# A two-layer decoder: scattering additions by tile, expert stores on another queue, a context term made once an entry

## What is computed

```python
# layer 0, routed experts: 8 experts, each takes up to 640 tokens (top 2 of the router)
hmid = relu(einsum('ceh,ehi->cei', inputs_tokens, experts_inter))
out = einsum('cei,eih->ceh', hmid, experts_out)
combined = zeros((T, h)).at[used_tokens].add((out * weights).reshape(-1, h))

# layer 1, coattention: c is x, q is the context, 77 rows
cq = einsum('bcd,bqd,d->bcq', c, q, w_cq) + b_cq
s = (c @ w_c + b_c)[:, :, None] + (q @ w_q + b_q)[:, None, :] + cq
a = softmax(s, axis=2)
b_att = softmax(max(s, axis=2), axis=1)

# layer 1, gated experts: 16 experts, each takes 32 tokens of every entry
h = gelu(einsum('becd,edf->becf', expert_in, w1) + b1)
expert_out = einsum('becf,efd->becd', h, w2) + b2
out = out.at[arange(b)[:, None, None], idx].add(gates[..., None] * expert_out)
```

## Time and profile before

| what | value |
|---|---|
| median of 3 runs | 2429.12 us (2428.93 to 2432.93) |
| the profiled execution, its own time | 2436.9 us |
| its span, first to last instruction | 2435.0 us |
| TensorE busy, of the span | 2087.2 us, 86% |
| VectorE, ScalarE, GpSimd busy | 64%, 52%, 46% |
| mean granted TensorE clock | 0.933 of full speed |
| routed experts | about 820 to 1059 us of the span |
| coattention | about 1416 to 1597 us |
| gated experts | about 1687 us to the end |

### The profile page before, as it was taken

How to read it: one execution, slowest core, us unless ns; L and a number is a source line. 1 busy time by engine, 2 the same in 40 slices (tenths; PEclk the granted TensorE clock), 3 DMA queues, 4 the chain that set the end, 5 groups by cost and what they waited for, 6 DMA issues and landing times. The chain is left out here.

```text
span 2435.0 us, 47109 instructions
## 1 busy us (share of the span) xinstructions
PE 2087.2 (86%) x17414; PEld 1478.5 (61%) x17446; DVE 1565.7 (64%) x3061; ACT 1267.3 (52%) x2042; POOL 1126.5 (46%) x1292
## 2 busy tenths in 40 slices
PE   7599999995995499948999979951999999999995
PEld 5466666663663388735666668841667676676664
DVE  5488888875896655537888746666554554555542
ACT  2366666663443355626666634432664655646642
POOL 2988888841220243236665213301454554545533
PEclk9799999997998699979999969975999999999998
DMA  5000000000002233211111000041343444444422
GB/s 223 1 2 1 0 0 0 0 1 6 10 6 70 93 127 144 76 37 36 27 26 26 1 14 16 13 138 72 104 95 100 95 106 97 84 103 104 102 47 33
DMA packets 63078, 135.99 MB, mean 56 GB/s; under 512 B 11201, under 2 KB 47249, under 8 KB 56081
## 3 DMA queue, kind: packets, MB, share of 16 engines
q0 software_dynamic: 31488, 52.45, 10.8%
q1 hardware_dynamic: 31504, 82.41, 9.7%
HBM read 100.22 MB, written 34.60 MB: 55 GB/s over the span
## 5 line engine op out<-in xcount | busy, mean ns | idle before, releaser
L3354 ACT ACTIVATE f_h<-bank,f_b 128x512 f32<-128x512 f32 x256 | 175.9, 687 | 276.3 <-PE bank L176 269.0
L3397 DVE TENSOR_TENSOR f_hidlo<-f_h,f_hidhi 128x512 f16<-128x512 f32 x256 | 177.2, 693 | 169.1 <-ACT f_hidhi L3355 169.1
L176 PE MATMUL ring<-f_w2hi,f_hidhi 128*128 128x256 f16 x1024 | 279.2, 273 | 6.3 <-DVE f_hidlo L3397 4.1
L176 PE MATMUL ring<-f_w2hi,f_hidlo 128*128 128x256 f16 x1024 | 279.1, 273 | 0.0
L176 PE MATMUL ring<-f_w2lo,f_hidhi 128*128 128x256 f16 x1024 | 279.1, 273 | 0.0
L3453 POOL DMA_INDIRECT out<-f_y,f_to_row x128 | 212.0, 1656 | 47.5 <-issue 34.1
L176 PE MATMUL bank<-f_xthi,f_w1hi 128*128 128x512 f16 x512 | 194.7, 380 | 0.0
L176 PE MATMUL bank<-f_xtlo,f_w1hi 128*128 128x512 f16 x512 | 194.6, 380 | 0.0
L176 PE MATMUL bank<-f_xthi,f_w1lo 128*128 128x512 f16 x512 | 194.6, 380 | 0.0
L3355 ACT ACTIVATE f_hidhi<-bank,f_b 128x512 f16<-128x512 f32 x256 | 173.9, 679 | 0.0
L3439 POOL DMA_INDIRECT f_xg<-tokens,f_from_row x128 | 149.6, 1169 | 47.9 <-issue 34.5
(11 more groups left out here) (620 smaller groups left out, 6047.9 us busy)
## 6 DMA issues: line engine op xcount, KB each, us to landing
f_raw<-in_e_w SPq DMA_DIRECT2D x32, 1024.0 KB, 4.9
c_raw<-in_e_w SPq DMA_DIRECT2D x16, 1024.0 KB, 4.9
slots_out<-c_y POOLq DMA_DIRECT2D x40, 128.0 KB, 3.5
x<-in_x SPq DMA_DIRECT2D x1, 4096.0 KB
tokens<-c_xn SPq DMA_DIRECT2D x16, 256.0 KB, 2.6
tokens<-f_xn SPq DMA_DIRECT2D x16, 256.0 KB, 2.4
out<-x SPq DMA_DIRECT2D x1, 4096.0 KB, 14.3
wb<-in_wb SPq DMA_DIRECT2D x1, 3096.0 KB, 33.0
```

The source lines that it names most:

```text
L176: mm = pe.matmul(out, left[a], right[b], start=first and n == 0, stop=last and n == 2)
L3354: act.activation(h32[n % 4][:, :], src, ACT.Gelu_apprx_tanh, bias=bias).then_inc(sig["h_full"], 1)
L3397: dve.tensor_tensor(hid_v[1][:, it, at], h32[n % 4][:, :], hid_v[0][:, it, at], ALU.subtract).then_inc(sig["h_lo"], 1)
```

## The change

It has three edits. In the gated experts GpSimd waits for the tile that it is about to add, not for all eight, and copies `to_row` ahead of that. In the routed experts the stores are issued by SyncE, woven between the loads of the expert after next; VectorE waits for `y_stored` itself, and `y_free` falls away. In coattention the context's term is made once per twin, by two matmuls at the head of the pair, into columns of their own in the same bank (`by_context`); ScalarE copies them to SBUF (`row`), and VectorE adds them with the biases while it takes `similar`. TensorE waits for `row_ready` ahead of `similar`.

```diff
--- before.py
+++ after.py
@@ -1946,13 +1946,32 @@
         with nc.Block() as block:
             @block.sync
             def _(sp):
-                def load(p, e, more):
+                def load_w1(e):
                     sp.wait_ge(sig["w1_split"], e.before)
                     sp.dma_start(raw1[:, :], dram["e0_w1"][bass.ds(e.before * P, P), :]).then_inc(sig["w1_loaded"], 16)
+                def load_w2(e):
                     sp.wait_ge(sig["w2_split"], e.before)
                     sp.dma_start(raw2[:, :], dram["e0_w2"][bass.ds(e.before * P, P), :]).then_inc(sig["w2_loaded"], 16)
 
-                each_expert(sp, E0, load)
+                def expert(p, e, more):
+                    after = Turn(value(sp, e.before + 2), value(sp, e.before + 3)) if more == 2 else None
+                    if after:
+                        load_w1(after)
+                    for ct in range(CT):
+                        sp.wait_ge(sig["y_read"], e.count(CT, ct + 1))
+                        sp.dma_start(dram["slots_out"][bass.ds(e.before * CAP0 + ct * P, P), :],
+                                     tiles(y[p][:, :], CT)[:, ct, :]).then_inc(sig["y_stored"], 16)
+                        if ct == 0 and after:
+                            load_w2(after)
+                for e in (Turn(0, 1), Turn(1, 2)):
+                    load_w1(e)
+                    load_w2(e)
+                each_expert(sp, E0, expert)
+                sp.wait_ge(sig["y_stored"], 16 * E0 * CT)
 
             @block.tensor
             def _(pe):
@@ -2067,7 +2086,7 @@
                         after = Turn(e.now, e.now + 1)
                         low_slots(after)
                         low_w1(after)
-                    dve.wait_ge(sig["y_free"], e.before)
+                    dve.wait_ge(sig["y_stored"], e.count(16 * CT, 0))
                     for ct in range(CT):
                         dve.wait_ge(sig["y_made"], e.count(CT, ct + 1))
                         dve.tensor_copy(y[p][:, ct * D:(ct + 1) * D], bank[4 + ct % 4][:, 0:D]
@@ -2099,18 +2118,10 @@
                 def expert(p, e, more):
                     if more == 2:
                         gather(Turn(e.after, e.after + 1))
-                    pool.wait_ge(sig["y_stored"], e.count(16 * CT, 0))
-                    pool.sem_inc(sig["y_free"], 1)
-                    for ct in range(CT):
-                        pool.wait_ge(sig["y_read"], e.count(CT, ct + 1))
-                        settle(pool, sig)
-                        pool.dma_start(dram["slots_out"][bass.ds(e.before * CAP0 + ct * P, P), :],
-                                       tiles(y[p][:, :], CT)[:, ct, :]).then_inc(sig["y_stored"], 16)
 
                 gather(Turn(0, 1), first=True)
                 gather(Turn(1, 2))
                 each_expert(pool, E0, expert)
-                pool.wait_ge(sig["y_stored"], 16 * E0 * CT)
 def linear_attention(nc, mem, dram):
 
 
@@ -2738,7 +2749,7 @@
             u = Twin(sig, p)
             u.bank = mem.banks[4 * p:4 * p + 4]
             u.c_t, u.c_n, u.sim_w = sb("c_t", KT * CTX), sb("c_n", D), sb("sim_w", KT * CTX)
-            u.a, u.a_t = sb("a", NT * CTX), sb("a_t", S)
+            u.a, u.a_t, u.row = sb("a", NT * CTX), sb("a_t", S), sb("row", CTX)
             u.neg_peak, u.total = sb("neg_peak", NT), sb("total", NT)
             u.top, u.e_row, u.e_sum = sb("top", 1), sb("e_row", S), sb("e_sum", 1)
             u.b_col, u.q2c, u.tmp = sb("b_col", NT), sb("q2c", KT), sb("tmp", W2)
@@ -2754,6 +2765,7 @@
             u.turned, u.peak_row = u.bank[0], u.bank[0][0:1, 0:S]
             u.b_out, u.q2c_out = u.bank[0][:, S:S + NT], u.bank[0][:, S + 8:S + 8 + KT]
             u.similar, u.a_turned = u.bank[1][:, 0:NT * CTX], u.bank[1][0:CTX, S:2 * S]
+            u.by_context = u.bank[1][:, NT * CTX:(NT + 1) * CTX]
             u.c2q_out, u.out = u.bank[2], u.bank[3]
             twins.append(u)
 
@@ -2800,21 +2812,24 @@
                                 product(twins[m // 6], 1 - q, ago, m // 3 % 2, m % 3)
 
                     for u in twins:
+                        pe.wait_ge(u["sim_w_ready"], i.now)
+                        pe.wait_ge(u["a_t_ready"], i.before)
+                        for h in range(KT):
+                            mm = pe.matmul(u.by_context, wq_v[:, h, :], u.c_v[:, h, :], start=h == 0, stop=h == KT - 1)
+                        mm.then_inc(u["row_made"], 1)
+                    for u in twins:
                         pe.wait_ge(u["xn_ready"], i.now)
                         pe.wait_ge(u["q2c_read"], i.before)
                         transpose_entry(pe, mem, u.turned, u.xn[q][:, :]).then_inc(u["xn_transposed"], 1)
                     products(0)
                     for u in twins:
                         pe.wait_ge(u["xn_t_ready"], i.now)
-                        pe.wait_ge(u["sim_w_ready"], i.now)
-                        pe.wait_ge(u["a_t_ready"], i.before)
+                        pe.wait_ge(u["row_ready"], i.now)
                         for t in range(NT):
                             out = u.similar[:, t * CTX:(t + 1) * CTX]
                             for h in range(KT):
-                                pe.matmul(out, u.xt_v[q][:, h, t * P:(t + 1) * P], u.sw_v[:, h, :], start=h == 0,
-                                          stop=False)
-                            for h in range(KT):
-                                mm = pe.matmul(out, wq_v[:, h, :], u.c_v[:, h, :], start=False, stop=h == KT - 1)
+                                mm = pe.matmul(out, u.xt_v[q][:, h, t * P:(t + 1) * P], u.sw_v[:, h, :], start=h == 0,
+                                               stop=h == KT - 1)
                         mm.then_inc(u["similar"], 1)
                     products(1)
                     for u in twins:
@@ -2876,6 +2891,10 @@
 
                 def pair(q, i, ago, more):
                     for u in twins:
+                        act.wait_ge(u["row_made"], i.now)
+                        act.wait_ge(u["neg_peak_ready"], i.before)
+                        act.activation(u.row[:, :], u.by_context, ACT.Copy).then_inc(u["row_ready"], 1)
+                    for u in twins:
                         act.wait_ge(u["xn_transposed"], i.now)
                         if ago is not None:
                             act.wait_ge(u["out_made"], ago.before)
@@ -2961,7 +2980,9 @@
                 def pair(q, i, ago, more):
                     for u in twins:
                         dve.wait_ge(u["similar"], i.now)
-                        order.step(dve.tensor_scalar(u.a[:, :], u.similar, b_sum[:, :], None, ALU.add))
+                        order.step(dve.scalar_tensor_tensor(out=u.a_v, in0=tiles(u.similar), scalar=b_sum[:, :],
+                                                            in1=u.row[:, :].unsqueeze(1).to_broadcast([P, NT, CTX]),
+                                                            op0=ALU.add, op1=ALU.add))
                         order.wait()
                         dve.wait_ge(u["peak_row"], i.before)
                         dve.tensor_reduce(u.neg_peak[:, :], u.a_v, AX.X, ALU.max, negate=True
@@ -3444,12 +3465,13 @@
 
                     pool.wait_ge(sig["added"], e.count(16 * CT, 0))
                     pool.sem_inc(sig["y_free"], 1)
-                    pool.wait_ge(sig["y_ready"], e.count(CT, CT))
                     settle(pool, sig)
                     pool.tensor_copy(to_row[:, :], rows[:, bass.ds(e.before * EB, EB)]).then_inc(sig["to_ready"], 1)
                     pool.wait_ge(sig["to_ready"], e.now)
                     settle(pool, sig)
                     for ct in range(CT):
+                        pool.wait_ge(sig["y_ready"], e.count(CT, ct + 1))
+                        settle(pool, sig)
                         pool.indirect_dma_start(out, bass.IndirectOffsetOnAxis(ap=to_row[:, ct:ct + 1], axis=0),
                                                 y[p][:, ct * D:(ct + 1) * D], None, compute_op=ALU.add
                                                 ).then_inc(sig["added"], 16)
```

## The result

The changed kernel takes 2398.1 us, the kernel before 2431.0 on the same chip: a ratio of 0.986 (0.984 to 0.987). By the ratio that is 34.8 us less (31.6 to 37.9); the two medians differ by 32.9.

The account below looks back on a forecast made before the run. The chain was taken as TensorE in both expert stages, eight scattering additions at the end, and TensorE and VectorE alternating in coattention. Savings of 13.6 + 0.4 + 10.2 = 24.2 us from 2429.12 gave 2404.9 us, range 2400 to 2415.

Parts of the forecast that it names:

- Scattering additions: End of the gated experts: only the eighth addition is left after VectorE's last `f_y`, 13.6 us less (13.0 to 14.0).
- The stores: End of the routed experts: stores issued by SyncE instead of GpSimd gain a faster reaction, 0.4 us (-0.4 to 0.6).
- At the end of the stage GpSimd's 0.59 us becomes SyncE's reaction: Behind the routed experts' last copy: SyncE reacts faster than GpSimd, landing taken as the same 2.0 us; 0.4 us gained.
- The estimate of 0.8: Routed experts' last store: the hardware queue's earlier first byte would gain 0.4 us more, 0.8 in all.
- Coattention: Eight pairs: six steady ones give 8.4 us, the first 1.8, the second nothing; 10.2 us less (2 to 14).
- 0.89 - 0.47 = 0.42 us is left: Head of four steady pairs: two added matmul groups cost 0.89 us and fill TensorE's 0.47 us wait for the `q2c` copies.
- VectorE allows 1.06 + 0.64 = 1.7 and 0.75 + 0.64 = 1.39: Steady pairs: VectorE's wait plus TensorE's slack before the peaks caps the gain at 1.7 or 1.39 us by kind.
- A: Rival, chance 0.11: VectorE holds coattention, TensorE's wait moves to the peaks, only the first pair's 1.8 us remains; 2413 us.
- B: Rival, chance 0.04: coattention's `e_a` queues behind GpSimd's bias addition, 18 us on top; 2423 us.
- C: Rival, chance 0.03: TensorE's clock rises later in coattention, some 17 us more per late pair; two late give 2439 us.
- D: Rival, chance 0.03: the scattering additions don't come off tile by tile and pile up at the end; 2418.5 us.

## Why the prediction fell short, point by point

**Scattering additions: right.** 13.6 us predicted, 13.4 found. GpSimd's reaction was taken as 0.59 us and was 0.79 (2390.99 to 2391.78). That the additions cost nothing in the loop held too.

**The stores: the gain that was priced is there, a cost of 6.6 us was left out, and this is the larger half of the error.** The step that failed is "At the end of the stage GpSimd's 0.59 us becomes SyncE's reaction": it priced what comes ahead of the store and ended the stage with its landing. Its own part is as it says, and a little more: SyncE begins 0.02 us after the copy, and the last store lands in 1.7 us, 0.57 + 0.3 = 0.87 us. (The estimate of 0.8 that the prediction worked out from the Trainium skill, DMA: Bandwidth & Descriptors, Latency and other measured facts, comes nearer to that than my 0.4; the step of 0.4 us between the two queues' first bytes in it is 0.3 here, from landing to landing.) The other 6.6 us are the drain. They could have been seen: the stage's store lands at 1060.46, the next part starts at 1068.27, and nothing in the argument spoke of the 7.8 us between. The Trainium skill (VectorE: DVE Perf Modes, The DRAIN you can't avoid) gives about 12 ns, on every engine, for the drains that the runtime puts ahead of a kernel and behind it. Those here end a block of the program itself, and that figure is no guide to them: GpSimd's behind the routed experts took 0.46 to 14.0 us.

**Coattention: right in kind, 13 us instead of 10.2.** All of the lack is in the steady pairs: 10.9 us (11.9 against the one profile with a slow fifth pair) where 8.4 stood. The first two pairs gave 1.6 to 1.9 us, as forecast (1.8). Three steps of the term:

- The similarity became 3.53 - 1.75 = 1.78 us shorter (1508.60 to 1512.13 before, 1495.88 to 1497.63 now), as predicted.
- The step "0.89 - 0.47 = 0.42 us is left" should read 0.85 - 0.64 = 0.21: the row took 0.85 us (1511.19 to 1512.04), and the wait it fills was worth 0.64. That is 0.2 us more than forecast in each of the four pairs.
- The step "VectorE allows 1.06 + 0.64 = 1.7 and 0.75 + 0.64 = 1.39" bound the two pairs with the long wait to 1.39. Both bounds were taken with VectorE and TensorE leaving `q2c` together. Now TensorE turns `xn` 0.28 us after the copies end (1511.76 to 1512.04), for 0.08 before, and by these rows VectorE gains the difference; and the 1.39 came from pairs that a late load had stretched, and that load is no longer late. They gained 2.63 us: 1.11 from the late load (20.97 to 19.86 without it), 1.52 from the shorter work. The 1.11 are luck: the edit was not meant to move the third pair's fetch, and the fifth pair was slow by chance.

**The clock: chance, nearly balanced.** The first profile's coattention is 17.5 us shorter, and its linear attention and norm 3.1 longer. Windows of the changed kernel, the norm, then the first pair in two pieces:

```profile
1388.00:1413.30 25.30, 15.47 (x113) 8.83 (x110) 6.51 (x18) 4.76 (x9) 0.00 (x0) 0.51 0.00 1
...
1422.70:1429.50 6.80, 4.62 (x33) 3.48 (x33) 4.75 (x19) 3.98 (x12) 2.49 (x2) 1.00 0.05 12
1429.50:1439.80 10.30, 10.30 (x43) 9.44 (x43) 6.56 (x13) 5.67 (x13) 4.76 (x4) 0.50 0.08 23
```

In the kernel before, where the same work stands some 3 us later, its first half was still near the upper level:

```profile
1388.00:1402.00 14.00, 10.71 (x138) 7.03 (x140) 6.00 (x10) 5.36 (x8) 0.00 (x0) 0.93 0.00 1
```

So the clock fell sooner ahead of coattention and stood at the upper level for 6.8 us of the first pair. Neither came back as such in the five later profiles with the new coattention (42.2 to 42.4 us from the first matmul to the third pair in four, 41.0 in one, 38.3 here). Taken together they are worth about a microsecond: coattention's 17.5 less the 13 to 13.7 of the edit, less the 3.1. The kernel with the added drain and the old coattention had such an early rise too (41.3 us for 44), so it is not a matter of the change.

**The rivals.** A: no; no wait at the peaks in the steady pairs. B: no; `e_a` takes 0.36 to 0.38 us. C: no; 1.00 from 1439.8 on. D: no; the additions stand 2.62 us apart. The routed experts' period stayed 27.9 us.

**The sum, put right.** 13.4 + 7.5 + 13 = 33.9 us; measured 34.8 (31.6 to 37.9), and 32.3 and 34.1 in the two repeats. The range failed because its low end took each term at the most that its mechanism allowed, and one mechanism, the drain, was missing.

## What to carry to other kernels

Between a part's last transfer and the next part's first instruction, account for every microsecond: a gap that no row explains can be a cost with an owner, here GpSimd's drain. An engine that has issued many transfers is worth a try at ending its part early or draining while it is idle; here the gaps got shorter by it, by 6.1 and 2.7 us, and the whole times could not show the 2.7. A wait that one fills is worth the distance from the last start to the next, less what an unbroken row of the same work takes, not the idle time that the view prints. Before a wait seen in two of six repeats becomes a bound, look at what else ran in just those two.

## What the runs showed that was not expected

- GpSimd's drain took 3.3 us after 40 gathers, 6.6 after 40 gathers and 40 stores, 0.46 after 5 stores, 0.71 after 8 additions, but 3.49 after the gated experts' 256 transfers. Right behind the same 40 gathers, beside the other engines' work, it took 7.0 us from the end of the last gather (13.7 in its record), and 3.3 when it came 60 us later. Coattention's block, in which GpSimd issues no transfer, ends with one of 2.05 us. So the length is not simply proportional to the transfers; what sets it stays open.
- One instruction fetch of 16 KB beside a 77 KB load made the load 0.7 to 1.0 us longer, and a shift of 64 instructions took it away. In the shifted kernel a fetch met the part's first two loads of `c_t` instead, which took 3.7 and 2.8 us. TensorE's first matmul stood 10.3 us after the start of coattention there, for 5.2 before, and the one run as a whole took 2462.1 us, longer than each of nine of the kernel before (2442.4 to 2456.9). Not every fetch beside a load costs this: in the changed kernel one that began 0.55 us ahead of a load (1441.53 and 1442.08) left it at 2.0 us.
